# GpSimd's indirect transfers: the bound named from a register set once per function instead of given as a number each time

## What is computed

```python
edge_index = jnp.stack([src, dst])
x = x + _L0_gnn_ref(_layernorm(x), edge_index, W_l, W_r, att, bias)   # attention over a node's edges
x = x + _L0_ffn_ref(_layernorm(x)[None], Wr, br, W1, b1, W2, b2)[0]   # 8 experts, the best one
x = x + _L1_gnn_ref(_layernorm(x), edge_index, W, b)                  # normalised sum over a node's edges
x = x + _L1_ffn_ref(_layernorm(x)[None], hash_proj, W1, W2)[0]        # 64 experts of limited room, two per token
```

## Time and profile before

| | us |
|---|---|
| median of 3 runs | 2886.7 (2885.25 to 2890.72) |
| span of the profiled execution, first to last instruction | 2733.6 |
| median less that span: what lies around the span | 153.1 |

### The profile page before, as it was taken

One profiled execution on the slowest core, in us unless ns is written; L12 is line 12 of the kernel. 1 busy time (PEld: TensorE's weight loads), 2 busy tenths in 40 slices (PEclk: granted clock), 3 DMA queues, 4 the chain that ended last, 5 costly groups with the idle time before them and its releaser, 6 DMA issues. The chain is left out here.

```text
span 2733.6 us, 43338 instructions
## 1 busy us (share of the span) xinstructions
PE 2118.0 (77%) x11528; PEld 1261.1 (46%) x11554; DVE 1837.2 (67%) x5188; ACT 988.2 (36%) x2224; POOL 1794.8 (66%) x2144
## 2 busy tenths in 40 slices
PE   8999999957787738999978969999998377774000
PEld 3444444435565526665644426666665244452000
DVE  4776776645555569999951116777777388886675
ACT  1111111115555515777773425555555122220000
POOL 3555555567777458887737755777777667664776
PEclk9999999978999959999999989999999599997555
DMA  5755555548999746888749976666664599996999
GB/s 198 232 190 178 191 184 182 193 147 271 307 314 312 258 154 193 256 260 262 238 180 324 409 285 211 214 220 215 212 214 138 179 342 371 366 338 242 371 383 360
DMA packets 331876, 689.90 MB, mean 252 GB/s; under 512 B 48217, under 2 KB 55347, under 8 KB 331505
## 3 DMA queue, kind: packets, MB, share of 16 engines
q1 hardware_dynamic: 220088, 404.15, 42.7%
q0 software_dynamic: 76720, 218.39, 24.5%
q10 hardware_dynamic: 34825, 64.59, 6.4%
HBM read 416.71 MB, written 287.44 MB: 258 GB/s over the span
## 5 line engine op out<-in xcount | busy, mean ns | idle before, releaser
L2122 POOL DMA_INDIRECT xg<-n_rows,ids x219 | 219.0, 1000 | 109.6 <-PE psum L154 61.6
L148 PE MATMUL psum<-wl,xT 128*128 128x512 f32 x632 | 288.8, 600 | 0.0
L148 PE MATMUL psum<-wg,yT 128*128 128x512 f32 x632 | 285.5, 595 | 0.0
L148 PE MATMUL psum<-wr,xT 128*128 128x512 f32 x632 | 284.1, 592 | 0.0
L337 ACT ACTIVATE xb<-xa,xsc 128x512 f32<-128x512 f32 x79 | 64.2, 814 | 480.3 <-POOL xsc L397 480.3
L384 POOL TENSOR_TENSOR ve<-mv,epst 128x1 f32<-128x1 f32 x79 | 51.1, 647 | 254.1 <-DVE mv L439 254.1
L1688 POOL DMA_INDIRECT slot_tokens<-sl x158 | 169.1, 1070 | 70.9 <-issue 66.9
L2295 POOL DMA_INDIRECT q<-slot_outputs,qs x158 | 167.8, 1062 | 72.3 <-issue 47.8
L154 PE MATMUL psum<-ident,xg 128*128 128x128 f32 x876 | 136.4, 294 | 92.9 <-DVE gT L2236 73.4
L148 PE MATMUL psum<-wc,x1T 128*128 128x264 f32 x632 | 162.8, 402 | 35.0 <-DVE hb L1231 27.4
L148 PEld LDWEIGHTS psum<-wr,xT 128*128 128x128 f32 x632 | 120.1, 190 | 151.2 <-issue 151.2
(11 more groups left out here) (323 smaller groups left out, 5316.5 us busy)
## 6 DMA issues: line engine op xcount, KB each, us to landing
slot_outputs<-yo ACTq DMA_DIRECT2D x54, 1024.0 KB
x_rows<-x SPq DMA_DIRECT2D x158, 256.0 KB, 3.2
edge_sums<-eo SPq DMA_DIRECT2D x29, 1056.0 KB, 6.5
edge_sums<-go SPq DMA_DIRECT2D x29, 1024.0 KB
xT<-in_xTt SPq DMA_DIRECT2D x79, 256.0 KB
xl_rows<-xl SPq DMA_DIRECT2D x79, 256.0 KB
xr_rows<-xr SPq DMA_DIRECT2D x79, 256.0 KB
residual_rows<-xb SPq DMA_DIRECT2D x79, 256.0 KB, 3.8
```

The lines of the kernel that those rows point to most:

```text
L148: last = nc.tensor.matmul(ps, lhs[:, k, :], rhs[:, k, :], start=(k == 0), stop=(k == DK - 1))
L2122: pool.indirect_dma_start(xg[:, t % 8, :], None, XN3, bass.IndirectOffsetOnAxis(ids[:, t:t + 1], 0), bounds_check=NP - 1, oob_is_err=False ...
```

## The change

Each of these GpSimd functions puts its bound into a register once, and its transfers name the register. The waits stay where they were written. Cut to its core:

```diff
@@ edge stage
+                row_limit = pool.to_reg(NP - 1)
                 for w in range(ET):
                     if w >= 16:
                         pool.wait_ge(b_v, w - 15)
                     pool.indirect_dma_start(gl[:, w % 16, :], None, XL, bass.IndirectOffsetOnAxis(idx[:, 0, w:w + 1], 0),
-                                            bounds_check=NP - 1, oob_is_err=False).then_inc(b_gl[w % 16], 16)
+                                            bounds_check=row_limit, oob_is_err=False).then_inc(b_gl[w % 16], 16)
...
@@ expert stage
                 pool.memset(zrow[:], 0.0).then_inc(z_0, 1)
+                row_limit = pool.to_reg(NP - 1)
                 for t in range(LISTED):
                     if t >= 8:
                         pool.wait_ge(p_tr, t - 7)
                     pool.indirect_dma_start(xg[:, t % 8, :], None, XN3, bass.IndirectOffsetOnAxis(ids[:, t:t + 1], 0),
-                                            bounds_check=NP - 1, oob_is_err=False).then_inc(p_ld[t % 8], 16)
+                                            bounds_check=row_limit, oob_is_err=False).then_inc(p_ld[t % 8], 16)
...
```

More of the change, by code:

```diff
@@ L690, in _ @@
                     pool.indirect_dma_start(gr[:, w % 8, :], None, XR, bass.IndirectOffsetOnAxis(idx[:, 1, w:w + 1], 0),
-                                            bounds_check=NP - 1, oob_is_err=False).then_inc(b_gr[w % 8], 16)
+                                            bounds_check=row_limit, oob_is_err=False).then_inc(b_gr[w % 8], 16)
             @block.vector
@@ L1059, in _ @@
             def _(pool):
+                sum_limit = pool.to_reg(NONE)
                 def edge_rows(t):
@@ L1063, in edge_rows @@
                     pool.indirect_dma_start(ai[:, t % 12, :], None, EO, bass.IndirectOffsetOnAxis(nodeq[:, t:t + 1], 0),
-                                            bounds_check=NONE, oob_is_err=False).then_inc(c_le[t % 12], 16)
+                                            bounds_check=sum_limit, oob_is_err=False).then_inc(c_le[t % 12], 16)
                 def average(t):
@@ L1430, in _ @@
                     pool.indirect_dma_start(gg[:, w % 8, :], None, GR, bass.IndirectOffsetOnAxis(idx[:, 0, w:w + 1], 0),
-                                            bounds_check=NP - 1, oob_is_err=False).then_inc(d_ld[w % 8], 16)
+                                            bounds_check=row_limit, oob_is_err=False).then_inc(d_ld[w % 8], 16)
             @block.vector
@@ L1674, in _ @@
                                    pattern=[[1, MH], [-1, MH]], channel_multiplier=0).then_inc(e_lo, 1)
+                sum_limit = pool.to_reg(NONE)
+                slot_limit = pool.to_reg(ME * SLOTS * P - 1)
                 def edge_rows(t):
@@ L1680, in edge_rows @@
                     pool.indirect_dma_start(ea2[:, t % 8, :], None, EO2, bass.IndirectOffsetOnAxis(nodeq[:, t:t + 1], 0),
-                                            bounds_check=NONE, oob_is_err=False).then_inc(e_le[t % 8], 16)
+                                            bounds_check=sum_limit, oob_is_err=False).then_inc(e_le[t % 8], 16)
                 def enter(t):
@@ L1688, in enter @@
                         pool.indirect_dma_start(IDXF, bass.IndirectOffsetOnAxis(sl3[:, k, t:t + 1], 0),
-                                                sl3[:, 2, t:t + 1], None, bounds_check=ME * SLOTS * P - 1,
+                                                sl3[:, 2, t:t + 1], None, bounds_check=slot_limit,
                                                 oob_is_err=False).then_inc(e_id[0], 16)
@@ L2288, in _ @@
             def _(pool):
+                slot_limit = pool.to_reg(LISTED * P)
                 for b in range(NG4):
@@ L2296, in _ @@
                                                     bass.IndirectOffsetOnAxis(qs[:, b % 3, t % 4, k:k + 1], 0),
-                                                    bounds_check=LISTED * P, oob_is_err=False)\
+                                                    bounds_check=slot_limit, oob_is_err=False)\
                                 .then_inc(q_ld[b % 3], 16)
```

## The result

The changed kernel takes 2854.2 us in the median (2851.1 to 2858.8, four runs), the kernel before beside it 2888.7 (2885.3 to 2893.4). The ratio is 0.9888, 95% interval 0.9871 to 0.9905: 32 us faster by the ratio and 34.5 by the medians, where no change that can be told was forecast (2884.5, and 2878.5 to 2890.5 as the range). The forecast was wrong.

The account below looks back on a forecast made before the run. Bounds were read by stage: DMA in second edge, expert and last, VectorE in node, TensorE in routing, POOL never alone. From 2886.7 us, less 2.4 plus 0.2 for remaining moves, gave 2884.5; range 2878.5 to 2890.5.

Parts of the forecast that it names:

- around the span: Whole execution: 153.1 us between the trace's 2733.6 us span and the 2886.7 us median, left as they are.
- Part 1: All stages: 1,040 moves of 29 ns go, 30.2 us of sequencer time; 512 transfers where the sequencer runs ahead costed at nothing.
- The rival that put the move into the gap: POOL-paced stages: each transfer loses 0.029 us to its move; edge stage gives 6.8 us, reaching 2879.9; chance 0.04.
- Part 2: Where POOL stands idle for a wait: the wait moves from move to transfer, gaining 0.4 us each, bounds +0.08 and -0.74.
- the prompt release: Rival, expert and routing stages: transfer starts as soon as the copy, 0.74 us a wait, 7.8 us in all, 2878.9; chance 0.13.
- The rival by which the wait costs on the transfer: Two edge stages: 322 transfers pay 0.078 us for carrying a wait, 25.1 us slower, 2911.8; chance 0.06.
- What of it reaches the end: Expert stage 3.6 us (nine waits) and routing stage 1.2 us at 0.4 us a wait; half of 4.8 taken, 2.4 us.
- What was to show it: Profile after: moves 1,047 to 7, gap 0.30 us, six stages within 3 us; wrong if expert stage over 6 us shorter.

Follow-up runs that it names:

- the second trace: The kernel before, unchanged, run again to get a trace of an execution as long as the timed ones: 2901.3 us, ratio 1.0003.
- moves_ahead: Against the kernel before: all 1,040 moves stay, each written ahead of the wait, which the transfer then carries; ratio 0.9912.
- ring12: Twelve expert-stage gather buffers in place of eight, in the kernel before (ratio 1.0013) and in the changed kernel (0.9889), both against the kernel before.

## Why the prediction was wrong

**The base.** The prediction's first step failed ahead of its sum: one execution's span, some 150 us shorter than any timed run, was taken for the usual one, and the difference was put "around the span". It lay in the stages. All three views that settled the case came from that trace: DMA at 0.96 in the expert stage (0.93 over the whole stage, and 0.85 in the second trace), 61 held waits of 61.6 us (114.1), and TensorE stopped by VectorE's copy for 72.1 us (30.5). In the edge stage the unusual trace had GpSimd behind, held ten times for 3.0 us; in the second trace `gl` is held 24 times, 68 us:

```profile
POOL gl L686 <- DVE vv L741: 68.1, 24, 4.3
```

**Part 1 was right.** The moves cost nothing that these runs can tell: moves_ahead keeps them all and has the gain (0.9912, 0.9890 to 0.9933, against 0.9888), and the gap is 0.30 us without them. The rival that put the move into the gap falls with it.

**Part 2 was right in kind and near in size.** The wait's new place is the whole effect that these runs can tell, by 0.50 us a held release, where 0.4 was taken from between +0.08 and -0.74. Of the 0.73 us between copy and gather 0.50 are gone. The whole 0.74 us, the most that the bounds allowed and what the prompt release counted on, does not come: 0.23 us are left, by the pairs above. The rival by which the wait costs on the transfer falls: back to back, transfers that carry a wait still have 0.30 or 0.31 us ahead of them, as at 2508.13.

**"What of it reaches the end" failed.** It counted only waits for the gathered rows, nine of 5.6 us, and came to 2.4 us. That TensorE does not wait for those rows is true, and ring12 shows it. The conclusion was wrong: a release reaches the end without such a wait, by the timelines once in every group of four. At 0.50 us and 54 groups this term is 27 us, not 2.4, and 20 to 25 were measured. That the release's place is the cause is shown in the expert stage; why nothing behind it takes up the delay stays open. The edge stage, costed at nothing since GpSimd seemed to run without waits there, gave 9.3. The rival of the prompt release had the right cause, a transfer that starts sooner behind its release (by 0.50 us), and 0.13 of the chance, but took its size from the same nine waits.

**What was to show it.** The moves fell from 1,047 to 7 and the gap stayed, as expected. The stages did not stay within 3 us, and the sentence on what would be wrong, an expert stage more than 6 us shorter, names what came.

## What to carry to other kernels

Compare the span of a trace with the times ahead of everything else: here a span lies 1.6 to 1.8 us below the time of its own execution, and where the two differ by far more, as the 153.1 us did, the trace is of another execution than those that are timed, and its waits are not theirs. Ask of each wait which instruction carries it: a register move ahead of a transfer takes the wait and puts 0.50 us behind every release here, and it is enough to move it ahead of the wait (ratio 0.9912), or to name a register (0.9888). And a release's delay can be on the path of a loop though nobody waits for the data that it brings, as 20 to 25 us of the expert stage show; count how often a release is held in one turn of the loop, and multiply for a first estimate.

## What was not expected of the hardware

TensorE stops among its transposes with no wait in the trace, for 54.1 us in the expert stage of the kernel before, again, and 0.5 in the unusual trace of the same program. In the first, the semaphore of a group's first product comes 2.85 us after the product's modelled end, in the second 0.04. The Gelu that waits for it starts 0.66 to 1.12 us after the end of GpSimd's last transfer, by the changed kernel's trace. One execution of the program ran the expert stage in 353 us and another in 409; two kernels that leave this stage as it was took 408.7 and 410.5. No run here says why.
